# Attention: in even steps, half a projection directly behind the burst of value matmuls, not at the end of the step

## The chip, the cores and the metric

The kernel runs on one core of a Trainium2 chip. The metric is the device time of one execution in microseconds (us), from the start to the end of the program on that core; the median of several runs is compared.

## What is computed

One decoder layer in float32. Self-attention over `x` (2 x 2048 x 512, 16 heads of 32), then cross-attention to a short context, then a feed-forward network with 8 experts, each followed by a residual sum and a layer norm. Only the first of the three matters here:

```python
qkv = x @ qkv_w + qkv_b
q, k, v = ...                                   # 16 heads of 32
attn = softmax(einsum('bnhd,bmhd->bhnm', q, k) * scale)
out = einsum('bhnm,bmhd->bnhd', attn, v)
```

The output projection, the cross-attention and the experts come later in the same program and are the same before and after.

## The kernel before

The program is one long sequence for each engine, written out in Python loops, with semaphores between them. Self-attention takes the first 2,000 us or so, the rest the experts for the most part.

**Units, chunks, steps.** Four heads make a group of 128 rows, and a batch and a group make a unit: `UNITS` = 8. A unit has `NQ` = 4 chunks of 512 queries, so there are `CHUNKS` = 32 chunks. A chunk is walked in `T` = 16 steps `kt`, one for each 128 keys, and a step in `HG` = 4 turns `i`, one for each head.

**What TensorE does in a turn** (`chunk`, L781 to L804). It issues one matmul of the maxima for a chunk further on (`max_pass`, L675, tile `sa_mx`) and one matmul of scores for this chunk (`score`, L745, tile `sa_sc`). Both write 512 columns and read fp32r operands. The pass of maxima computes query by key and VectorE reduces its bank with `reduce_max` (L556), from three banks in turn. From the maxima come the shifts of the softmax: once a chunk VectorE makes them (`make_shift`, L564), TensorE transposes them into a bank of maxima in step 13 (`transpose_shift`, L683), VectorE copies them out (`leave_shift`, L576) and SyncE's queue moves them into `q_stack` for the next chunk.

**Scores.** A matmul of scores writes one of two banks in turn. ScalarE takes the exponential of each (L515, tile `sa_prob`), and score `n` waits until exponential `n - 2` is done (`after(pe, prob_ready, n - 1)`, L747).

**The burst** (`burst`, L729). In every even step, after the second score (turn 1), TensorE adds up the values of the two steps before: 8 matmuls of 32 output columns each, four of them side by side in the array (L696, tile `sa_pv`, 16 records in a trace). Where `kt % 4 == 2` four more such matmuls make the row sums of the softmax (`row_sums`, L700, tile `sa_den`, 8 records). These are float32 operands. GpSimd adds the probabilities of four steps up beforehand (L310), with VectorE's help (`add_pair`, L558).

**The projections.** While one unit is attended to, the queries, keys and values of the next are projected. One projection of 128 rows by 512 tokens is a job: 4 parts over the channels, each in `HALVES` = 2 halves, in float32. A half is one matmul of 256 columns for a query or key job (L670, 2 records) and two matmuls of 128 columns for a value job (L664, 4 records). All jobs use one PSUM bank, `misc`, one after another. Each of the 28 chunks of units 0 to 6 has three jobs (`OPS`, L110), chunks 28 and 29 have one, the last two none. Where the halves stand is written out by hand:

```python
MID, END, HALVES = 1, HG - 1, 2
SLOTS = [(kt, at) for kt in range(T) for at in ((MID, END) if kt % 2 else (END,))]
PLACES = [SLOTS[:2] + SLOTS[:6], SLOTS[7:15], SLOTS[16:24]]
```

A slot is a step and a turn; the halves of the slot are issued at the end of that turn, in an even step at `MID` behind the burst (L803 comes after L798). The three entries of `PLACES` are the places of the first, second and third job of a chunk. A finished job is read out of its bank by ScalarE (`leave_high`, L459) and VectorE (`leave_psum`, L536) at the turn in `LEFT_AT`: for the first job in step 4, for the second in step 10, for the third in step 0 of the next chunk, all in turn 1. A query or key is then moved into its stack by 12 DMAs of SyncE's queue (`move_stack`, L270). In step 13 TensorE waits before turn 0 for the stacks that chunk `g + 2` needs (L784 to L789).

**Order of the other engines.** ScalarE, VectorE and GpSimd each walk the same steps and turns in their own list; ScalarE reads the bank of values out in turn 2 of step 0 (`leave_pv`) and the bank of row sums in turn 2 of step 2 (`leave_den`). VectorE inverts the row sums in steps 8 and 12 (`invert`, L582).

Of the kernel before, what the change touches and what calls it, by code (L numbers as in the profile page):

```python
# [75 lines left out]
def self_attention(nc, z, keep, block, x, xT_dram, qkv_w, qkv_b, attnT_dram, rows_dram):  # L76


    B, N, C, KC, G, HG, D, T, NQ = z.B, z.N, z.C, z.KC, z.G, z.HG, z.D, z.T, z.NQ
# [32 lines left out]
           Op("k", 3, 1, 2, 5), Op("q", 0, 1, 2, 6), Op("v", 3, 1, 2, 5),  # L112
           Op("v", 0, 1, 3, 6), Op("q", 1, 1, 3, 7), Op("v", 1, 1, 3, 7)]
    MID, END, HALVES = 1, HG - 1, 2
    SLOTS = [(kt, at) for kt in range(T) for at in ((MID, END) if kt % 2 else (END,))]
    PLACES = [SLOTS[:2] + SLOTS[:6], SLOTS[7:15], SLOTS[16:24]]
    PLACES[0].sort()
    LEFT_AT = ((0, 4, MID), (0, 10, MID), (1, 0, MID))

# [12 lines left out]
    JOBS = [Job(0, what, n, None, None, None, None) for what, n in FIRST_OPS]  # L132
    JOBS += [Job(u + o.ahead, o.what, o.n, u * NQ + o.c, u * len(LOADS) + o.load, PLACES[i % 3], LEFT_AT[i % 3])
             for u in range(UNITS) for i, o in enumerate(OPS) if u + o.ahead < UNITS]
# [686 lines left out]
def cross_attention(nc, z, keep, block, tail, a):  # L821


    B, N, C, KC, M, E, CAP = z.B, z.N, z.C, z.KC, z.M, z.E, z.CAP
    SLOTS, NT, SKIP = z.E * z.CAP, z.TOK // P, 2 ** 20
    W = C + 2
# [18 lines left out]
    with ExitStack() as ctx:  # L845
# [272 lines left out]
        def _(pool):  # L1118
# [24 lines left out]
            def send_rows(n):  # L1143
# [8 lines left out]
                for t in range(TQ):  # L1152
                    pool.indirect_dma_start(a.rows, bass.IndirectOffsetOnAxis(ap=skip_i[:, par, t:t + 1], axis=0),
                                            x2[par][:, t, :], None, bounds_check=SLOTS - 1, oob_is_err=False).then_inc(scattered, 16)

# [1095 lines left out]
def decoder_layer(nc, x, ctx_rows, qkv_w, qkv_b, proj_w, proj_b, Wq, Wk, Wv, Wo, bo, gx, bx, gl, bl,  # L2251
                  router_w, w1, b1, w2, b2, out):
    z = Shapes(x, ctx_rows, w1)
    slots = z.E * z.CAP

    def scratch(name, shape, dt=F32):
        return nc.dram_tensor(name, shape, dt, kind="Internal").ap()

    xT = scratch("xT", (z.B, z.C, z.N))
    attnT = scratch("attnT", (z.B, z.C, z.N))  # L2260

    rows = scratch("rows", (slots, z.C + 2))
    a = Tensors()
    a.x, a.ctx, a.attnT, a.out = x, ctx_rows, attnT, out
    a.proj_w, a.proj_b, a.Wq, a.Wk, a.Wv, a.Wo, a.bo = proj_w, proj_b, Wq, Wk, Wv, Wo, bo
    a.gx, a.bx, a.gl, a.bl, a.rw = gx, bx, gl, bl, router_w
    a.w1, a.b1, a.w2, a.b2 = w1, b1, w2, b2
    a.rows = rows

    a.wqk = scratch("wqk", (z.C, z.XH * z.M))  # L2270
    a.vw = scratch("vw", (z.XH * z.M, z.C))
    with ExitStack() as ctx:
        a.counts = Stage(nc, ctx, "keep").sb("counts", [P, z.E], I32)
        with ExitStack() as keep:

            block = keep.enter_context(nc.Block())
            tail = self_attention(nc, z, keep, block, x, xT, qkv_w, qkv_b, attnT, rows)
            cross_attention(nc, z, keep, block, tail, a)
        experts(nc, z, a)
# [29 lines left out]
```

## Time and profile before

| | us |
|---|---|
| median of 3 runs (3521.16 to 3531.86) | 3529.65 |
| the profiled execution | 3527.62 |
| its span, first to last instruction | 3525.9 |
| TensorE (PE) busy, whole span | 3342.4 (95%) |
| VectorE (DVE) busy | 2646.1 (75%) |
| GpSimd (POOL) busy | 1809.5 (51%) |
| ScalarE (ACT) busy | 1703.4 (48%) |

The span and the profiled execution's own time differ by 1.7 us, which lie around the first and last instruction. PE is the stream of matmuls; their ends are modelled, so a busy PE may hold short waits, and the distance from the start of one matmul to the start of the next is the better measure. PEld are the loads of weights, which run beside matmuls. The mean granted TensorE clock is 0.976 of full speed.

### The profile page before, as it was taken

The page shows a single profiled execution, that of the slowest core. Times are in us where ns is not written, and L with a number is a line of the kernel's source. Part 1 is how long each engine was busy: PE and PEld are TensorE (multiplying, and loading weights), DVE is VectorE, ACT ScalarE, POOL GpSimd, SP SyncE. Part 2 cuts the span into 40 slices and gives each one's busy share as a digit, 9 for nine tenths or more (in the row PEclk, how much of TensorE's full clock was granted, in tenths as well). Part 3 has the DMA queues.
Part 4 walks back from the last instruction along what each step waited for, and adds up shares of the span by engine and source line. Part 5 has one row for each costly group of instructions (what it writes and reads, how often), then busy time and mean ns, then how long its engine had stood idle before and what let it go on. Part 6 is the DMA issues. An engine that isn't in the chain of part 4 may idle for free. (4 is left out here: it accounts for less than half of the span.)

```text
span 3525.9 us, 51323 instructions
## 1 busy us (share of the span) xinstructions
PE 3342.4 (95%) x18533; PEld 2356.0 (67%) x18533; DVE 2646.1 (75%) x4578; ACT 1703.4 (48%) x3101; POOL 1809.5 (51%) x884
## 2 busy tenths in 40 slices
PE   7999999999999999999999987999949999999996
PEld 6655566566666556656655445887739888988886
DVE  5888888888888888888888835888734765566667
ACT  2565665656655655656656653444312332233333
POOL 2587888888888888888888930011110101100111
PEclk9999999999999999999999998999969999999998
DMA  6321322322322322213211032132132333323332
GB/s 219 113 63 46 102 60 76 96 58 80 87 61 70 94 63 79 85 52 102 71 52 39 8 112 67 57 116 96 49 117 92 126 125 100 121 84 126 121 116 100
DMA packets 190280, 308.52 MB, mean 88 GB/s; under 512 B 25513, under 2 KB 72233, under 8 KB 190010
## 3 DMA queue, kind: packets, MB, share of 16 engines
q1 hardware_dynamic: 166970, 243.82, 22.4%
q0 software_dynamic: 14592, 44.32, 3.6%
q10 hardware_dynamic: 8448, 16.78, 1.4%
q8 instruction: 169, 2.77, 0.3%
q14 instruction: 101, 0.83, 0.1%
HBM read 195.66 MB, written 61.33 MB: 73 GB/s over the span
## 5 line engine op out<-in xcount | busy, mean ns | idle before, releaser
L556 DVE TENSOR_REDUCE sa_part_max<-sa_mx 128x1 f32<-128x512 f32 x2048 | 1311.3, 685 | 316.9 <-PE sa_mx L680 272.2
L515 ACT ACTIVATE sa_prob<-sa_sc 128x512 f32<-128x512 f32 x2010 | 1105.2, 595 | 684.9 <-PE sa_sc L748 671.0
L310 POOL TENSOR_TENSOR sa_quad_sum<-sa_quad_sum,sa_prob 128x1024 f32<-128x1024 f32 x500 | 1270.6, 2563 | 133.7 <-ACT sa_prob L515 131.8
L680 PE MATMUL sa_mx<-sa_k_even,sa_q_stack 96*128 96x512 f32 x1024 | 480.9, 473 | 15.0 <-DMA sa_q_stack<-sa_hilo 5.9
L2126 PE MATMUL ex_h<-ex_xT,ex_w 128*128 128x384 f32 (+2 forms) x2688 | 457.2, 325 | 29.6 <-issue 23.1
L680 PE MATMUL sa_mx<-sa_k_odd,sa_q_stack 96*128 96x512 f32 x1024 | 468.6, 458 | 9.8 <-DMA sa_q_stack<-sa_hilo 5.8
L2126 PEld LDWEIGHTS ex_h<-ex_xT,ex_w 128*128 128x128 f32 x2688 | 437.7, 191 | 43.6 <-issue 34.0
L310 POOL TENSOR_TENSOR sa_quad_sum<-sa_prob 128x1024 f32<-128x1024 f32 x126 | 300.2, 2383 | 234.7 <-ACT sa_prob L515 234.7
L2148 PE MATMUL ex_acc<-ex_w,ex_hT 128*128 128x512 f32 x1719 | 418.1, 394 | 0.0
L748 PE MATMUL sa_sc<-sa_q_stack,sa_k_even 98*128 98x512 f32 x1024 | 410.7, 401 | 0.0
L748 PE MATMUL sa_sc<-sa_q_stack,sa_k_odd 98*128 98x512 f32 x986 | 401.1, 409 | 1.4 <-ACT sa_prob L515 1.2
L2148 PEld LDWEIGHTS ex_acc<-ex_w,ex_hT 128*128 128x128 f32 x1719 | 319.2, 189 | 61.4
L1963 ACT ACTIVATE ex_h<-ex_h,ex_b 128x384 f32<-128x384 f32 x256 | 145.5, 580 | 345.9 <-PE ex_h L2126 345.8
L680 PEld LDWEIGHTS sa_mx<-sa_k_even,sa_q_stack 96*128 96x128 f32 x1024 | 195.5, 192 | 155.3 <-issue 101.6
L680 PEld LDWEIGHTS sa_mx<-sa_k_odd,sa_q_stack 96*128 96x128 f32 x1024 | 193.9, 189 | 152.9 <-issue 107.3
L1889 POOL DMA_DIRECT2D ex_xg<-rows x48 | 26.5, 556 | 509.0 <-PE ex_h L2111 506.9
L696 PE MATMUL sa_pv<-sa_prob,sa_v_odd 128*32 128x512 f32 x2048 | 249.1, 602 | 1.0 <-ACT sa_prob L515 1.0
L696 PE MATMUL sa_pv<-sa_prob,sa_v_even 128*32 128x512 f32 x2048 | 246.2, 598 | 0.0
L748 PEld LDWEIGHTS sa_sc<-sa_q_stack,sa_k_odd 98*128 98x128 f32 x986 | 187.0, 190 | 79.2 <-ACT sa_prob L515 55.3
L748 PEld LDWEIGHTS sa_sc<-sa_q_stack,sa_k_even 98*128 98x128 f32 x1024 | 195.1, 191 | 46.0 <-ACT sa_prob L515 19.7
L2075 DVE CAST ex_hT<-ex_h 128x384 fp32r<-128x384 f32 x256 | 94.5, 369 | 133.6 <-ACT ex_h L1963 132.9
L1141 POOL TENSOR_TENSOR ca_rstd<-ca_var_eps,ca_minus_half 128x8 f32<-128x8 f32 x16 | 26.5, 1654 | 324.4 <-DVE ca_var_eps L1209 324.4
(229 smaller groups left out, 4078.2 us busy)
## 6 DMA issues: line engine op xcount, KB each, us to landing
ex_w_in<-in_L_ffn_w_dram SPq DMA_DIRECT2D x130, 512.0 KB, 4.5
sa_xT<-xT SPq DMA_DIRECT2D x57, 1024.0 KB, 5.2
sa_q_stack<-sa_hilo SPq DMA_DIRECT2D x372, 64.0 KB, 2.0
rows<-sa_empty SPq DMA_DIRECT2D x48, 257.0 KB, 3.9
ex_rows<-rows POOLq DMA_DIRECT2D x8, 1542.0 KB, 7.7
sa_k_odd<-sa_hilo SPq DMA_DIRECT2D x192, 64.0 KB, 2.0
ex_xg<-rows POOLq DMA_DIRECT2D x48, 256.0 KB, 3.0
sa_k_even<-sa_hilo SPq DMA_DIRECT2D x168, 64.0 KB, 2.0
```

Of the source, the lines that this page charges most:

```text
L310: pool.tensor_tensor(quad_sum[:, i % 2, heads, :], so_far, prob[:, k, heads, :], ALU.add).then_inc(quad_ready, 1)
L515: act.activation(prob[:, kt % 4, j, :], score_bank(n)[:, :], ACT.Exp, scale=SCALE).then_inc(prob_ready, 1)
L556: dve.reduce_max(part_max[:, q, j, k:k + 1], max_bank(max_turn(n))[:, :], AX_X).then_inc(max_read, 1)
L680: pe.matmul(max_bank(max_turn(n))[:, :], q_stack[0:QK, j, at:at + P], k_stack[g // NQ % 2][0:QK, j, k * BANK:(k + 1) * BANK], start=True, ...
L696: last = pe.matmul(pv[D * j:D * (j + 1), :], v[buf][:, kt, D * j:D * (j + 1)], prob[:, kt % 4, j, :], start=(kt == 0), stop=(kt == T - 1))
L748: pe.matmul(score_bank(n)[:, :], k_stack[g // NQ % 2][0:AUG, j, kt * P:(kt + 1) * P], q_stack[0:AUG, j, g % NQ * BANK:(g % NQ + 1) * BANK] ...
L1141: pool.tensor_tensor(rstd[:, which, :, :], var_eps[:, which, :, :], minus_half[:, :, :], ALU.pow).then_inc(rstd_ready, 1)
L1889: pool.dma_start(xg[:, t, :], a.rows[row:row + P, 0:C]).then_inc(gathered, 16)
L1963: act.activation(h[:, j % 2, half * HALF:(half + 1) * HALF], h_bank[half][:, 0:HALF], ACT.Gelu, bias=b1[:, step:step + 1]).then_inc(h_read ...
L2075: dve.tensor_copy(hT[:, j % 2, 0, cols], h[:, j % 2, cols]).then_inc(hT_hi, 1)
L2126: last = pe.matmul(h_bank[half][:, 0:slots], w1[:, i % 2, pw, k, :], xT[:, e % 2, px, k, half * HALF:half * HALF + slots], start=(part == ...
L2148: last = pe.matmul(acc[t][:, :], hT[:, i % 2, ph, t * P:(t + 1) * P], w2[:, i % 2, pw, :], start=(i == 0 and part == 0), stop=(i == STEPS ...
```

## The change

```diff
-    SLOTS = [(kt, at) for kt in range(T) for at in ((MID, END) if kt % 2 else (END,))]
-    PLACES = [SLOTS[:2] + SLOTS[:6], SLOTS[7:15], SLOTS[16:24]]
+    SLOTS = [(kt, at) for kt in range(T) for at in ((MID, END) if kt % 2 else (MID,))]
+    PLACES = [SLOTS[1:4] + SLOTS[1:6], SLOTS[7:15], SLOTS[16:24]]
     PLACES[0].sort()
```

The slots of even steps go from turn 3 to turn 1, where they stand behind the burst. Written out, with (step, turn):

| job | places before | places after |
|---|---|---|
| first | (0,3) (0,3) (1,1) (1,1) (1,3) (2,3) (3,1) (3,3) | (1,1) (1,1) (1,3) (1,3) (2,1) (2,1) (3,1) (3,3) |
| second | (5,1) (5,3) (6,3) (7,1) (7,3) (8,3) (9,1) (9,3) | (5,1) (5,3) (6,1) (7,1) (7,3) (8,1) (9,1) (9,3) |
| third | (11,1) (11,3) (12,3) (13,1) (13,3) (14,3) (15,1) (15,3) | (11,1) (11,3) (12,1) (13,1) (13,3) (14,1) (15,1) (15,3) |

No instruction, wait or DMA is added or removed. The last half of every job stays where it was, and so do the turns at which the jobs are read out.

## Rows read from the trace of the kernel before

**Rows 1.** The page: TensorE's busy tenths in 40 slices of 88 us.
```profile
PE   7999999999999999999999987999949999999996
```

**Rows 2.** Timeline of TensorE, the bursts of chunk 9: start us, us, engine, line, operation.
```profile
670.60 1.92 PE L696 MATMUL sa_pv<-sa_prob,sa_v_even 128*32 128x512 f32 x16
...
678.56 1.92 PE L696 MATMUL sa_pv<-sa_prob,sa_v_even 128*32 128x512 f32 x16
...
686.53 1.92 PE L696 MATMUL sa_pv<-sa_prob,sa_v_even 128*32 128x512 f32 x16
...
693.46 1.92 PE L696 MATMUL sa_pv<-sa_prob,sa_v_even 128*32 128x512 f32 x16
...
701.42 1.93 PE L696 MATMUL sa_pv<-sa_prob,sa_v_even 128*32 128x512 f32 x16
...
708.52 1.92 PE L696 MATMUL sa_pv<-sa_prob,sa_v_even 128*32 128x512 f32 x16
...
716.34 1.93 PE L696 MATMUL sa_pv<-sa_prob,sa_v_even 128*32 128x512 f32 x16
...
724.56 1.92 PE L696 MATMUL sa_pv<-sa_prob,sa_v_even 128*32 128x512 f32 x16
...
732.54 1.92 PE L696 MATMUL sa_pv<-sa_prob,sa_v_even 128*32 128x512 f32 x16
```

**Rows 3.** Timeline behind the burst of step 6 of chunk 9: a half at (6,3).
```profile
695.20 1.04 PE L704 MATMUL sa_den<-sa_quad_sum,sa_ones 128*32 128x512 f32 x8
...
696.17 0.19 PEld L680 LDWEIGHTS sa_mx<-sa_k_even,sa_q_stack 96*128 96x128 f32 x1 [0.84 <-issue]
696.17 0.50 PE L680 MATMUL sa_mx<-sa_k_even,sa_q_stack 96*128 96x512 f32 x1
...
696.51 0.39 PE L748 MATMUL sa_sc<-sa_q_stack,sa_k_even 98*128 98x512 f32 x1
...
696.98 0.40 PE L748 MATMUL sa_sc<-sa_q_stack,sa_k_even 98*128 98x512 f32 x1
...
697.21 0.59 PE L670 MATMUL sa_misc<-sa_xT,sa_wkv 128*128 128x256 f32 x2
...
697.88 0.40 PE L748 MATMUL sa_sc<-sa_q_stack,sa_k_even 98*128 98x512 f32 x1
```

**Rows 4.** Timeline behind the burst of step 10 of chunk 9: no half at (10,3).
```profile
712.01 2.28 ACT L515 ACTIVATE sa_prob<-sa_sc 128x512 f32<-128x512 f32 x4 [2.19 <-PE sa_sc L748]
712.05 0.40 PE L748 MATMUL sa_sc<-sa_q_stack,sa_k_even 98*128 98x512 f32 x1
...
712.66 0.19 PEld L748 LDWEIGHTS sa_sc<-sa_q_stack,sa_k_even 98*128 98x128 f32 x1 [0.42 <-ACT sa_prob L515]
712.67 0.51 PE L748 MATMUL sa_sc<-sa_q_stack,sa_k_even 98*128 98x512 f32 x1
...
713.25 0.40 PE L748 MATMUL sa_sc<-sa_q_stack,sa_k_even 98*128 98x512 f32 x1
```

**Rows 5.** Waits between 184 and 1948 us: waiter, releaser, us in total, times, longest.
```profile
PEld sa_sc L748 <- ACT sa_prob L515: 46.5, 153, 0.4
...
PE sa_mx L680 <- DMA sa_q_stack<-sa_hilo: 9.6, 14, 1.6
```

**Rows 6.** Timeline of VectorE and TensorE in steps 12 to 14 of chunk 9.
```profile
716.01 0.39 PE L748 MATMUL sa_sc<-sa_q_stack,sa_k_even 98*128 98x512 f32 x1
...
720.68 2.57 DVE L556 TENSOR_REDUCE sa_part_max<-sa_mx 128x1 f32<-128x512 f32 x4
...
723.16 0.67 DVE L580 CAST sa_shiftT<-sa_mx 8x512 fp32r<-8x512 f32 x1
...
723.89 0.50 PE L680 MATMUL sa_mx<-sa_k_even,sa_q_stack 96*128 96x512 f32 x1 [0.22 <-DVE sa_shiftT L580]
```

**Rows 7.** Timeline at step 13, turn 0 of chunk 11.
```profile
843.61 0.61 PE L664 MATMUL sa_misc<-sa_wkv,sa_xT 128*128 128x128 f32 x4
...
844.45 0.50 PE L680 MATMUL sa_mx<-sa_k_odd,sa_q_stack 96*128 96x512 f32 x1 [0.23 <-DMA sa_q_stack<-sa_hilo]
```

## The prediction

> **What bounds the kernel now.** First the page: TensorE is busy nine tenths or more in nearly every slice of self-attention [rows 1], so the length of this stage is what TensorE issues, plus the short waits between its matmuls that this digit can't show. So the next view is the timeline of TensorE, and in it the distance from burst to burst, since a half moves within such a period of two steps. Chunk 9 has bursts at 670.60, 678.56, 686.53, 693.46, 701.42, 708.52, 716.34, 724.56 and 732.54 us [rows 2], so the periods that begin with steps 0, 2, 4, ... 14 take 7.96, 7.97, 6.93, 7.96, 7.10, 7.82, 8.22 and 7.98 us. Each has the same 16 matmuls of maxima and scores and the same 8 of values; steps 2, 6, 10 and 14 have row sums besides, and the halves number 5, 3, 2, 3, 3, 2, 3, 3.
>
> The third view is what a half costs where it stands. Two scores without a half between them are 0.47 us apart (696.51, 696.98), with a half 0.90 (697.88) [rows 3], so a half takes **0.43** of TensorE's stream. Yet the period of step 8 (three halves) is only 0.17 longer than that of step 4 (two, none in turn 3 of the even step), and step 6 only 0.14 longer than step 10, the same pair with row sums [rows 2]. So a half at the end of an even step costs 0.14 to 0.17 net, and **0.26 to 0.29 us of it is cover for something else**. The timeline behind burst 10 shows what: the scores run 712.05, 712.67, 713.25, so 1.20 us for two distances where 0.94 would be TensorE's own pace, and the load of the first waits for an exponential [rows 4]. ScalarE needs 0.57 for one (2.28 for 4) against TensorE's 0.47 for a score and a maximum, and there are two banks; behind a burst the first two scores go out freely and the next two wait. A half in turn 3 of the even step stands exactly there and gives ScalarE the time. The list of waits has this one 153 times [rows 5]; it is small now because only steps 4 and 10 lack the half, and where no half comes at all.
>
> **The change, part by part.** Nothing is added or removed. The sum is over a chunk of 28 with three jobs.
>
> *The moved half itself.* Behind the burst it costs x, which no row shows. A burst ends with a hole: the row sums start at 695.20, 8 records of which four run together, and the next matmul at 696.17, 0.97 later, where two groups at the 0.43 of those in the burst would be 0.86; the score after it comes 0.34 later instead of 0.23 [rows 3]. I take it that the half meets the hole as the maximum does: its first record waits the 0.11, its second comes 0.34 later instead of 0.22, and the maximum behind it then follows at the normal pace. The hole is paid once, as before, and x = 0.43 + 0.01 to 0.02 = **0.45**. Bounds: if the hole's two parts (0.11 and 0.10) took the half in, x = 0.22; if a value job's four small records each met a late load once more, the 0.11 again, x = 0.56. I take 0.45, which is nearest the row of the maximum behind a burst.
>
> The row of the load is to be weighed against a rule. The load for the maximum behind the burst starts at 696.17 with its matmul, after 0.84 idle [rows 3]: it wasn't pulled ahead. The Trainium skill ("TensorE: Matmul & The Clock Gate", Part 2, what happens when you issue a matmul) says that the engine pulls weight loads ahead of running matmuls when they go to the background buffer. By that the half's load would be done by the end of the burst, and the total near the second rival's below; the trace does not agree for a load behind this burst.
>
> *Steps 6, 8, 14: one half each from turn 3 to behind the burst.* What is left between bursts is the period with two halves: 6.93 without row sums (step 4), 7.80 with (step 10, 7.82, or 6.93 + 0.86 = 7.79). Plus x: step 6 becomes 8.25 against 7.96, **+0.29**; step 8 7.38 against 7.10, **+0.28**; step 14 8.26 against 7.98, **+0.28**. What covered the moved half's time was ScalarE's lag, and that cover stays behind as a wait. Behind the burst ScalarE has long run dry (2.19 idle, [rows 4]), and so has VectorE, so the half covers nothing there.
>
> *Steps 0 and 2, the first job.* Two halves leave (0,3), one goes to (1,3), one to (2,1), and (2,3) goes to (2,1). Step 0 then holds four halves, all in step 1: 6.93 + 2 x 0.43 = 7.79 against 7.96, **-0.17**: a half less, and the wait is back. Step 2 holds two in the stretch and two behind the burst: 7.80 + 0.45 + 0.43 = 8.68 against 7.97, **+0.71**. ScalarE's reading of the row sums in that step ends no later than now.
>
> *Step 12.* Here VectorE leads in half of the chunks: its reductions run without a break, four in 2.57 us, then the copy of the shifts at 723.16, and TensorE's maximum at 723.89 waits for it [rows 6]. That chain starts with the first maximum behind the burst, as VectorE has run dry by then, so it moves by the whole of x: **+0.45**. In the other half TensorE waits before (13,0) for a stack's DMAs, 14 times in 28 chunks [rows 5]; in chunk 11 it could go on at 843.61 + 0.36 and goes on at 844.45, 0.48 later [rows 7]. The half at (12,3) and the half at (12,1) both lie ahead of this point, the DMAs start from step 10, which is unchanged, so the arrival moves by x - 0.43 only: **0**. Mean +0.22.
>
> *Queues and other waits.* The DMAs of the stacks, loads and shifts hang on the last halves and on the shifts. The former don't move; the shifts come up to 0.45 later in step 13 and are wanted two steps on, some 8 us. GpSimd's additions get more time, not less. Cost nothing. The first half of a first job waits for the bank at (1,1) instead of (0,3), later, so no new wait.
>
> *Sum:* 0.29 + 0.28 + 0.28 - 0.17 + 0.71 + 0.22 = 1.61 us a chunk, 28 times 45.1, and 2 x 0.54 for chunks 28 and 29, together **46 us**. On the profiled execution's 3527.62 that is 3574; this execution lies 2 us under the median of 3529.65, so 3574 to 3576. I say 3575.
>
> As a function of x a chunk changes by 4.5 x - 0.42: steps 2, 6, 8 and 14 hold one x each, step 12 half of one, and the second half of the pair in step 2 costs 0.43 whatever the hole. It breaks even at x = 0.09.
>
> **Rivals.**
> *The half fills the hole.* The weight load of a full-width float32 half is ready when the burst ends, and the two delays of 0.11 and 0.10 vanish in it: x = 0.22 to 0.24. Then 28 x (4.5 x 0.23 - 0.42) = 17 us, plus 1: about **3546**. For it: burst and half are both float32, the maxima are not. Against it: a half between two fp32r matmuls shows no delay at either change (0.90 - 0.47 is 0.43, two records at some 0.22 each), so it isn't the type that makes the hole but the change of width, which stays. Even if the 0.33 from the last score to the burst (716.01 [rows 6] to 716.34 [rows 2]) shrank to the usual 0.23 as well, x would be 0.13 and the end 3533. 10%.
> *The other side: no loss, or a gain.* The two periods in which I read the lag, those of steps 4 and 10, are also the ones in whose first turns ScalarE reads out a finished job besides its exponentials. If the late scores come of that and not of the missing half, the other steps have no lag to give back: steps 6, 8 and 14 change by x - 0.43 = +0.02 each, steps 0 and 2 together by as much, step 12 by up to half of 0.02. That is 28 x 0.1 = 3 us, **3531**, no change; with the hole filled too, 28 x 4.5 x 0.20 = 25 us less, 3503. It decides where ScalarE is still busy with the job when the first score behind the burst lands. Against it: it sat idle for 2.19 us before its first exponential behind burst 10 [rows 4], so the read was long over. 4%.
> *Dearer than forecast.* Each half behind a burst meets a second late load, above all the value jobs (three of four third jobs, steps 12 and 14), x = 0.56: 28 x 4.5 x 0.11 = 14; and the waits for stacks do not absorb step 12, 14 x 0.45 = 6 more: up to **3595**. 13%.
> That the change doesn't do what it says is excluded by the table of places; but note that the first job's two halves from step 0 don't all go behind a burst, and half of them go to step 1.
>
> **How the numbers follow.** My case 73%: x from 0.43 to 0.48, and the lag from 0.24 to 0.30, give 3568 to 3583. The range takes in part of the other cases: up to 3596, and down to 3553, since x may lie between hole and no hole in only some of the steps. A measurement of this kernel can tell about 0.3%, 10.6 us, from no change. Faster by over that needs both the hole and no lag, 2%; within it, the opposite rival by itself and the lower edge of the first, 5%; slower 93%.
>
> **What would show it.** In the timeline of the changed kernel: (1) step 8's period about 7.38 and step 6's 8.25; (2) behind each even burst the half's first record about 0.54 after the last group of values starts, its second 0.34 after that; (3) the third and fourth score behind every burst late, and the wait of score loads for exponentials about 300 to 400 times instead of 153; (4) step 0 shorter by 0.17, step 2 longer by 0.7; (5) the waits for stacks at (13,0) as now, 14 times. I am wrong if the period with a half behind the burst is within 0.05 of the present one: then either x is near 0.2 or ScalarE's lag was not the cover.

## The result, and the profile after

The changed kernel takes 3572.86 us (median of 4 runs, 3572.76 to 3576.62), the kernel before in the same session 3526.28 us (4 runs): ratio **1.013**, 95% interval 1.0117 to 1.0143, 46.6 us slower. The forecast was 3575 us, 3553 to 3596, slower. TensorE's granted clock was 1.00 in chunks 1 to 27 in both traces, so the clock has no part in the difference.

The page shows as little of it as before. Its line of TensorE's busy time, and the line of slices:

```profile
span 3571.1 us, 51323 instructions
...
PE 3387.2 (95%) x18533; PEld 2327.2 (65%) x18533; DVE 2624.6 (73%) x4578; ACT 1703.6 (48%) x3101; POOL 1807.3 (51%) x884
...
PE   7999999999999999999999987999949999999997
```

The same 18533 matmuls are "busy" 45 us longer. The record of a matmul of scores or maxima lasts some 0.40 us, and the next one is due 0.23 after its start, so a score that starts 0.14 late (0.61 after the last one instead of 0.47, as below) leaves no gap in the busy time. The starts of the bursts say more. TensorE's timeline of chunk 9, the counterpart of [rows 2]:

```profile
687.75 1.92 PE L696 MATMUL sa_pv<-sa_prob,sa_v_even 128*32 128x512 f32 x16
...
695.54 1.92 PE L696 MATMUL sa_pv<-sa_prob,sa_v_even 128*32 128x512 f32 x16
...
704.19 1.92 PE L696 MATMUL sa_pv<-sa_prob,sa_v_even 128*32 128x512 f32 x16
...
711.12 1.92 PE L696 MATMUL sa_pv<-sa_prob,sa_v_even 128*32 128x512 f32 x16
...
719.36 1.92 PE L696 MATMUL sa_pv<-sa_prob,sa_v_even 128*32 128x512 f32 x16
...
726.73 1.92 PE L696 MATMUL sa_pv<-sa_prob,sa_v_even 128*32 128x512 f32 x16
...
734.55 1.92 PE L696 MATMUL sa_pv<-sa_prob,sa_v_even 128*32 128x512 f32 x16
...
743.23 1.92 PE L696 MATMUL sa_pv<-sa_prob,sa_v_even 128*32 128x512 f32 x16
...
751.49 1.92 PE L696 MATMUL sa_pv<-sa_prob,sa_v_even 128*32 128x512 f32 x16
```

The periods are 7.79, 8.65, 6.93, 8.24, 7.37, 7.82, 8.68 and 8.26 us, against 7.96, 7.97, 6.93, 7.96, 7.10, 7.82, 8.22 and 7.98. Steps 4 and 10 stand still, every other one has moved. What happens inside is in the timeline behind the burst of step 8, which now has its half in front:

```profile
721.21 0.30 PEld L670 LDWEIGHTS sa_misc<-sa_xT,sa_wkv 128*128 128x128 f32 x2 [0.84 <-issue]
721.21 0.70 PE L670 MATMUL sa_misc<-sa_xT,sa_wkv 128*128 128x256 f32 x2
721.53 0.19 PEld L680 LDWEIGHTS sa_mx<-sa_k_even,sa_q_stack 96*128 96x128 f32 x1
721.56 0.59 PE L680 MATMUL sa_mx<-sa_k_even,sa_q_stack 96*128 96x512 f32 x1
...
721.99 0.39 PE L748 MATMUL sa_sc<-sa_q_stack,sa_k_even 98*128 98x512 f32 x1
...
722.42 1.78 ACT L515 ACTIVATE sa_prob<-sa_sc 128x512 f32<-128x512 f32 x3 [2.33 <-PE sa_sc L748]
722.46 0.39 PE L748 MATMUL sa_sc<-sa_q_stack,sa_k_even 98*128 98x512 f32 x1
...
723.07 0.19 PEld L748 LDWEIGHTS sa_sc<-sa_q_stack,sa_k_even 98*128 98x128 f32 x1 [0.42 <-ACT sa_prob L515]
723.07 0.50 PE L748 MATMUL sa_sc<-sa_q_stack,sa_k_even 98*128 98x512 f32 x1
...
723.64 0.42 PE L748 MATMUL sa_sc<-sa_q_stack,sa_k_even 98*128 98x512 f32 x1
```

Three things are to be seen. The load of the half starts with its first record, after the same 0.84 idle that the maximum's load had [rows 3]: nothing is pulled into the burst. The first score comes 2.63 after the burst's start (721.99 - 719.36), where in the kernel before it came 2.19 (718.53 against 716.34 in step 12 of chunk 9), so the half costs 0.44 in this place. In step 8 itself the kernel before has the same 2.19 (703.61 against the burst's 701.42 in [rows 2]):

```profile
703.61 0.39 PE L748 MATMUL sa_sc<-sa_q_stack,sa_k_even 98*128 98x512 f32 x1
```

And the third score is 0.61 behind the second and the fourth 0.57 behind the third, as in [rows 4]: the lag is back. In the list of waits, 184 to 1948 us as in [rows 5]:

```profile
PEld sa_sc L748 <- ACT sa_prob L515: 130.8, 430, 0.4
...
PE sa_mx L680 <- DMA sa_q_stack<-sa_hilo: 9.0, 14, 1.5
```

The wait for exponentials is there 430 times instead of 153, 277 more, although this stretch of time holds less than before of chunks 28 and 29, where the wait is frequent in both kernels. Over chunks 1 to 27 alone the traces have it 404 times against 108: two more in each of five periods of every chunk (0, 2, 6, 8 and 14), and 26 in all in step 12. The wait for DMAs is as it was, 14 times.

### The profile page after: what moved, and what is told of

Read it like the earlier page. It is cut to its first block and busy times, and to the rows that moved or that the text cites. A ratio compares the mean times of both kernels' runs of the same rounds, so it can differ in the third digit from the quotient of the medians.

```text
span 3571.1 us, 51323 instructions
## 1 busy us (share of the span) xinstructions
PE 3387.2 (95%) x18533; PEld 2327.2 (65%) x18533; DVE 2624.6 (73%) x4578; ACT 1703.6 (48%) x3101; POOL 1807.3 (51%) x884
## 5 line engine op out<-in xcount | busy, mean ns | idle before, releaser
L556 DVE TENSOR_REDUCE sa_part_max<-sa_mx 128x1 f32<-128x512 f32 x2048 | 1297.5, 684 | 379.2 <-PE sa_mx L680 347.2
L680 PE MATMUL sa_mx<-sa_k_even,sa_q_stack 96*128 96x512 f32 x1024 | 471.1, 464 | 15.3 <-DMA sa_q_stack<-sa_hilo 6.0
L680 PE MATMUL sa_mx<-sa_k_odd,sa_q_stack 96*128 96x512 f32 x1024 | 460.1, 449 | 9.7 <-DMA sa_q_stack<-sa_hilo 5.6
L748 PE MATMUL sa_sc<-sa_q_stack,sa_k_even 98*128 98x512 f32 x1024 | 422.2, 412 | 0.0
L748 PE MATMUL sa_sc<-sa_q_stack,sa_k_odd 98*128 98x512 f32 x986 | 409.3, 417 | 1.5 <-ACT sa_prob L515 1.5
```

The lines of the kernel that those rows point to most:

```text
L556: dve.reduce_max(part_max[:, q, j, k:k + 1], max_bank(max_turn(n))[:, :], AX_X).then_inc(max_read, 1)
L680: pe.matmul(max_bank(max_turn(n))[:, :], q_stack[0:QK, j, at:at + P], k_stack[g // NQ % 2][0:QK, j, k * BANK:(k + 1) * BANK], start=True, ...
L748: pe.matmul(score_bank(n)[:, :], k_stack[g // NQ % 2][0:AUG, j, kt * P:(kt + 1) * P], q_stack[0:AUG, j, g % NQ * BANK:(g % NQ + 1) * BANK] ...
```

## The experiments

The kernels are compared with the kernel before as it ran beside them: 3525.77 us for the two parts, the half ahead of the burst and the half left out; 3524.96 for the short exponentials and the quarters first; 3524.32 for the half in turn 2 and the half first. All are read by the same measure, the mean length of each period over chunks 1 to 27, worked out from the starts of the bursts in each trace (in us; the last column is the start of chunk 28 less that of chunk 1):

| kernel | 0 | 2 | 4 | 6 | 8 | 10 | 12 | 14 | chunks 1-27 |
|---|---|---|---|---|---|---|---|---|---|
| before | 7.98 | 7.97 | 6.93 | 7.95 | 7.10 | 7.82 | 8.73 | 7.99 | 1686.4 |
| after | 7.81 | 8.67 | 6.93 | 8.22 | 7.37 | 7.81 | 8.97 | 8.26 | 1729.1 |
| second and third jobs only | 7.98 | 7.97 | 6.93 | 8.22 | 7.37 | 7.81 | 8.81 | 8.26 | 1710.2 |
| first job only | 7.80 | 8.67 | 6.93 | 7.95 | 7.10 | 7.81 | 8.57 | 7.99 | 1696.1 |
| half ahead of the burst | 8.68 | 7.79 | 7.37 | 8.23 | 6.93 | 8.26 | 8.93 | 7.81 | 1727.8 |
| half at (8,3) left out | 7.98 | 7.97 | 6.93 | 7.95 | 6.93 | 7.82 | 8.70 | 7.99 | 1681.2 |
| short exponentials, old places | 7.98 | 8.08 | 6.70 | 8.08 | 7.10 | 7.59 | 8.83 | 7.99 | 1683.4 |
| short exponentials, new places | 7.59 | 8.44 | 6.70 | 8.08 | 7.14 | 7.58 | 8.90 | 8.03 | 1686.3 |
| half in turn 2 | 8.23 | 8.21 | 6.93 | 8.20 | 7.34 | 7.81 | 8.80 | 8.24 | 1721.3 |
| nine places, quarters first | 7.97 | 7.97 | 6.75 | 7.95 | 7.10 | 7.62 | 8.74 | 7.99 | 1676.1 |
| nine places, half first | 7.97 | 7.97 | 6.75 | 7.95 | 7.10 | 7.62 | 8.74 | 7.99 | 1676.2 |

Each row is one trace. The column of step 12 has a scatter of its own: in the half of the chunks that wait for DMAs it is 8.9 to 9.4 on average, from trace to trace, which alone moves the last column by up to 7 us. The start of chunk 1 lies between 170.3 and 175.2 us, in kernels whose programs differ little up to there.

### The change in two parts

```diff
+    BEHIND = [(kt, at) for kt in range(T) for at in ((MID, END) if kt % 2 else (MID,))]
-    PLACES = [SLOTS[:2] + SLOTS[:6], SLOTS[7:15], SLOTS[16:24]]
+    PLACES = [SLOTS[:2] + SLOTS[:6], BEHIND[7:15], BEHIND[16:24]]
```

> Only the second and third job of each chunk take the places behind the bursts; the first job keeps its old ones. Theory A (ScalarE's lag: a half in turn 3 of an even step covers 0.27 us of the wait for exponentials, and the same half behind the burst costs 0.44): steps 6, 8 and 14 longer by 0.26 to 0.28 each, step 12 by 0.43 in half of the chunks and 0 in the other half, so 1.0 us a chunk, 28 us, ratio to the kernel before 1.008. Theory B (the loss is of the first job, whose halves crowd in steps 1 and 2): no difference here, ratio 1.000 to 1.002.

3550.74 us, ratio 1.007 (1.0053 to 1.0087), 25 us. The other part, with `BEHIND` as above:

```diff
+    PLACES = [BEHIND[1:4] + BEHIND[1:6], SLOTS[7:15], SLOTS[16:24]]
```

> Only the first job takes its new places. Theory A: step 0 shorter by 0.17, step 2 longer by 0.70, so 0.53 a chunk, 16 us over 30 chunks, ratio 1.0045, and with the run of the other two jobs alone it adds up to the whole change. Theory B: nearly the whole loss is here, 40 us or more, ratio 1.011 to 1.013.

3540.28 us, ratio 1.0045 (1.0031 to 1.0059), 14.5 us. Each part moves its own periods, by as much as in the whole change, and no other; 25 and 14.5 make 39.5 of the 46.6; each part's interval reaches some 5 us to either side, so the 7 us between are not shown to be an effect. By period the parts add up for all but step 12, whose DMA waits differ between the traces. The loss is not one of the crowded first job alone: of the 39.5 us, five eighths come from the second and third job, which move single halves.

### The half ahead of the burst

```diff
                     score(g, kt, i)
+                    if kt % 2 == 0:
+                        for job, part in PARTS_AT.get((g, kt, i), ()):
+                            project_part(job, part)
                     if g < LAST or kt <= 2:
...
-                    for job, part in PARTS_AT.get((g, kt, i), ()):
-                        project_part(job, part)
+                    if kt % 2:
+                        for job, part in PARTS_AT.get((g, kt, i), ()):
+                            project_part(job, part)
```

> The changed kernel, but in even steps the half is issued ahead of the burst (behind the score of turn 1) instead of behind it. Theory A: neither place is where the scores lag, so the time is that of the changed kernel within 3 us, 3570 to 3576, with step 8 at 7.35 to 7.40 us. Theory C (what costs is that every engine that has run dry in the burst starts later by the half): ScalarE and VectorE work on during a half ahead of the burst, they start at once behind it, and most of the 46 us is gone: 3530 to 3540, step 8 near 7.1.

3571.6 us, ratio 1.0124 (1.0107 to 1.0141), the time of the changed kernel. My number for step 8 missed by bad bookkeeping: a half ahead of burst 8 counts in the period that begins with burst 6. So step 6 (with (8,1)) is 8.23, step 4 (with (6,1)) is 6.93 + 0.44 = 7.37, and step 8 is 6.93 without any. What the other engines do while TensorE is at the half makes no difference; that it isn't in turn 3 does.

### A half left out

```diff
         for part, at in enumerate(job.place or ()):
+            if at == (8, END):
+                continue
```

> The kernel before, with the half at (8,3) of each second job left out of the projection (its 256 columns lack one of four channel parts). Theory A: step 8 falls from 7.10 only to 6.93, by 0.17, although a half is 0.43 of the stream; the wait of score loads for exponentials rises by about 56 times; 28 chunks give 4 to 5 us less. Theory D (the lag in steps 4 and 10 comes of ScalarE reading out a job there, so other steps have none): step 8 falls by the whole 0.43 to 6.67, 12 us less.

Step 8 falls to 6.93, and the waits rise by 58, from 153 to 211. So work of 0.43 us, taken from an engine that in the kernel before is busy for 1671.01 of the 1686.40 us of chunks 1 to 27, was worth 0.17. Those chunks get 5.2 us shorter, where 27 x 0.17 is 4.6; the whole program ran once, in 3524.19 us, too near 3525.77 to tell. No job is read out in step 8, so the lag isn't a matter of steps 4 and 10: that is the rival of the other side gone. TensorE's timeline of chunk 9, bursts 8 and 10:

```profile
702.11 1.92 PE L698 MATMUL sa_pv<-sa_prob,sa_v_even 128*32 128x512 f32 x16
...
709.04 1.92 PE L698 MATMUL sa_pv<-sa_prob,sa_v_even 128*32 128x512 f32 x16
```

### Short exponentials, at the old and at the new places

```diff
-   act.activation(prob[:, kt % 4, j, :], score_bank(n)[:, :], ACT.Exp, scale=SCALE).then_inc(prob_ready, 1)
+   act.activation(prob[:, kt % 4, j, 0:BANK // 2], score_bank(n)[:, 0:BANK // 2], ACT.Exp, scale=SCALE).then_inc(prob_ready, 1)
```

The same edit is made to the kernel before and to the changed one. Both leave out half of every exponential, so they serve for the timing only.

> The kernel before with each exponential cut to 256 of its 512 columns (the other 256 keep old contents, so the attention is wrong); the places are the old ones. It takes the lag away by making ScalarE fast, some 0.35 us for one. Theory A: periods with a half at turn 3 stay (step 8 7.10, step 6 7.96), those without fall by 0.26 (step 4 to 6.67, step 10 to 7.54). Rival (the late scores come of VectorE's maxima or of the weight loads): step 4 stays at 6.93.

> The changed kernel with the same short exponentials. Theory A: without the lag a half costs its 0.43 to 0.44 in either place, so step 8 comes to 7.10 to 7.12 instead of 7.37, and chunks 1 to 27 take the same time as with short exponentials and the old places within 3 us. Rival (the place behind the burst is dear in itself): the difference of 1.6 us a chunk, 43 us over chunks 1 to 27, stays, step 8 at 7.37.

An exponential now takes 0.385 us instead of 0.595. One run each, 3496.70 us and 3500.15. At the old places the two periods without a half in turn 3 fall by 0.23, the others with the lag covered don't gain. At the new places the six moved periods come down, step 8 to 7.14, and chunks 1 to 27 take 1686.3 us against 1683.4: of the **42.7 us that the change costs, 2.9 are left**. This is the run that decides: the same places, the same holes behind the bursts, and only the exponential shorter. The 2.9 flatter the case somewhat. Steps 2 and 6 were to stay at 7.97 and 7.96 at the old places and both went to 8.08, by another effect (last section), which lengthens the old-places kernel by 27 x (0.11 + 0.13) = 6.5 us. The periods that this effect leaves alone are the better witness: steps 8 and 14 lost 0.27 each by the change with full exponentials, and 0.04 each with short ones. A half costs about what it takes in either place, and nearly all of the loss was the lag. A little lag stays, too: step 4, which has one half less than step 8, takes 6.70 instead of 7.10 - 0.43 = 6.67. The timeline behind burst 8 of chunk 9 with short exponentials and the new places:

```profile
705.95 0.39 PE L748 MATMUL sa_sc<-sa_q_stack,sa_k_even 98*128 98x512 f32 x1
...
706.38 1.82 ACT L515 ACTIVATE sa_prob<-sa_sc 128x256 f32<-128x256 f32 x4 [2.56 <-PE sa_sc L748]
706.41 0.39 PE L748 MATMUL sa_sc<-sa_q_stack,sa_k_even 98*128 98x512 f32 x1
...
706.81 0.19 PEld L748 LDWEIGHTS sa_sc<-sa_q_stack,sa_k_even 98*128 98x128 f32 x1 [0.20 <-ACT sa_prob L515]
706.89 0.42 PE L748 MATMUL sa_sc<-sa_q_stack,sa_k_even 98*128 98x512 f32 x1
```

The third score is 0.48 behind the second instead of 0.61, nearly TensorE's own pace, but its load still waits for the first exponential. An exponential of 0.385 can't be too slow for a score every 0.47. Nor does ScalarE work without a break in the changed kernel when the full exponentials make TensorE wait. Three narrow windows of its timeline behind burst 8 of chunk 9 show the first three starts:

```profile
722.42 0.60 ACT L515 ACTIVATE sa_prob<-sa_sc 128x512 f32<-128x512 f32 x1 [2.33 <-PE sa_sc L748]
...
722.91 0.59 ACT L515 ACTIVATE sa_prob<-sa_sc 128x512 f32<-128x512 f32 x1
...
723.61 0.60 ACT L515 ACTIVATE sa_prob<-sa_sc 128x512 f32<-128x512 f32 x1
```

The second starts 0.49 after the first, before that one has ended; then ScalarE sits idle from 723.50 to 723.61, because the third score itself came late (723.07). So ScalarE can take an exponential every 0.49, close to TensorE's 0.47, and has time to spare while TensorE waits for a bank. What is waited for is the **round trip of a bank**: from the start of a score to the start of its exponential 0.43 (705.95, 706.38), then the exponential. With 0.60 that is 1.03, and the load of the score two on starts some 0.05 later, at 1.08, and its matmul with it; it would be wanted at 0.94. With 0.385 it is 0.82, and the load is at 0.86, in time for a matmul at 0.94. So the rows put the lag down to the round trip over two banks, and not to ScalarE's pace.

### The half in turn 2

```diff
-    SLOTS = [(kt, at) for kt in range(T) for at in ((MID, END) if kt % 2 else (END,))]
+    SLOTS = [(kt, at) for kt in range(T) for at in ((MID, END) if kt % 2 else (END - 1,))]
```

> The kernel before with the halves of even steps in turn 2 instead of turn 3, between the first and the second score behind the burst. Theory A (two banks; the third score waits for the first exponential, the fourth for the second): a half there leaves the third score free, but the fourth still comes one bank too early, so the wait of 0.14 us and the late weight load of 0.10 behind it return at the fourth: step 8 at 7.33 to 7.38, ratio 1.008 to 1.012. Rival (any place in the stretch gives ScalarE the time): step 8 at 7.10 to 7.15, ratio under 1.002.

3565.17 us, ratio 1.0115 (1.0099 to 1.013), step 8 at 7.34. One turn too early costs 41 us, nearly as much as the change's 46.6. The timeline behind burst 8 of chunk 9 shows the wait one score later, at the fourth:

```profile
714.28 0.40 PE L748 MATMUL sa_sc<-sa_q_stack,sa_k_even 98*128 98x512 f32 x1
714.51 0.59 PE L670 MATMUL sa_misc<-sa_xT,sa_wkv 128*128 128x256 f32 x2
...
715.18 0.39 PE L748 MATMUL sa_sc<-sa_q_stack,sa_k_even 98*128 98x512 f32 x1
...
715.65 0.40 PE L748 MATMUL sa_sc<-sa_q_stack,sa_k_even 98*128 98x512 f32 x1
...
716.26 0.19 PEld L748 LDWEIGHTS sa_sc<-sa_q_stack,sa_k_even 98*128 98x128 f32 x1 [0.41 <-ACT sa_prob L515]
716.26 0.50 PE L748 MATMUL sa_sc<-sa_q_stack,sa_k_even 98*128 98x512 f32 x1
```

The half covers only what is wanted right after it.

### Nine places for a job

Steps 4 and 10 lack the half in turn 3 because a job has eight halves and nine places. Here two places get a quarter each:

```diff
-    PLACES = [SLOTS[:2] + SLOTS[:6], SLOTS[7:15], SLOTS[16:24]]
+    PLACES = [SLOTS[:2] + SLOTS[:6], SLOTS[6:15], SLOTS[15:24]]
+    QUARTERS = 2 * HALVES
+    PLACES[0] = [at for at in PLACES[0] for _ in range(2)]
+    PLACES[1:] = [[at for n, at in enumerate(places) for _ in range(2 if n > 1 else 1)] for places in PLACES[1:]]
...
```

The rest of the edit makes `project_part` take any run of quarters. Quarters of one job that stand in the same turn go out as one piece, so the two halves at (0,3) of a query or key job, for one, are now one matmul.

> The kernel before, but the second and third job use nine places instead of eight, (4,3) and (10,3) too: the first two places get a quarter each (128 columns, or one of the two matmuls of a value), the other seven a half. The same work. Theory A: a quarter of 0.22 us in turn 3 covers most of the lag of 0.26, so step 4 goes from 6.93 to 6.70 to 6.75 and step 10 from 7.80 to 7.57 to 7.62; what step 10 gains is eaten by the wait for DMAs in step 13 in half of the chunks; 8 to 10 us less in all, ratio 0.9975. Rival (the lag is spread along the stretch, or small pieces cost more than they cover): ratio 1.000 or over.

3519.79 us against 3524.96, ratio **0.9982** (0.9973 to 0.9991). Step 4 is 6.75 and step 10 7.62, as forecast. Chunks 1 to 27 are 10.3 us shorter in the trace, the whole program 5.2 in the medians (interval 3.2 to 9.5). Where the other 5 us go is not shown; outside chunks 1 to 27 the traces with full exponentials differ by up to 5.7 us (1839.4 to 1845.1). It is a small gain, but it beats both kernels.

> As the run with quarters, but of the nine places the first, (4,3) and (10,3), gets a whole half and the two after it a quarter each. Theory A: the whole half covers the whole lag at the third score, a quarter of 0.22 suffices between the later pairs (ScalarE needs 1.14 for a pair, TensorE 0.94 + 0.22), so step 4 at 6.67 to 6.70 against 6.75 with the quarter first, step 10 at 7.54 to 7.58; 10 us less than the kernel before, ratio 0.997. Rival: the quarters leave a lag at their own places, step 4 at 6.75 or over.

The variant puts the whole half first and the quarters behind it (`1 if n in (1, 2) else 2`): 3519.79 us against 3524.32, again 0.9982, and step 4 again 6.75, not 6.67 to 6.70. Theory A missed here, and the rival's number holds. The timeline of this variant in steps 4 and 5 of chunk 9, with a quarter ahead of 691.42 and another ahead of 692.62:

```profile
691.42 0.42 PE L755 MATMUL sa_sc<-sa_q_stack,sa_k_even 98*128 98x512 f32 x1
...
691.83 0.19 PEld L755 LDWEIGHTS sa_sc<-sa_q_stack,sa_k_even 98*128 98x128 f32 x1 [0.19 <-ACT sa_prob L523]
691.91 0.41 PE L755 MATMUL sa_sc<-sa_q_stack,sa_k_even 98*128 98x512 f32 x1
...
692.62 0.40 PE L755 MATMUL sa_sc<-sa_q_stack,sa_k_even 98*128 98x512 f32 x1
...
693.01 0.19 PEld L755 LDWEIGHTS sa_sc<-sa_q_stack,sa_k_even 98*128 98x128 f32 x1 [0.19 <-ACT sa_prob L523]
693.10 0.41 PE L755 MATMUL sa_sc<-sa_q_stack,sa_k_even 98*128 98x512 f32 x1
```

A pair of scores takes 1.19 us (691.91 to 693.10). I had set 1.14 for a pair, half of four exponentials in 2.28, which has ScalarE's idle time between two pairs only once. TensorE's own 0.94 + 0.22 = 1.16 falls short of 1.19, so about 0.03 is lost at each of the two pairs with a quarter. That is most of the 0.08 by which 6.75 lies over 6.67.

## Why the prediction was right

The total (3575 against 3572.86) is right by its own steps, not by luck. Per period, forecast and measured mean of chunks 1 to 27: step 0 -0.17 and -0.17; step 2 +0.71 and +0.70; step 6 +0.29 and +0.28; step 8 +0.28 and +0.27; step 12 +0.22 and +0.24; step 14 +0.28 and +0.27. That is 1.61 and 1.58 a chunk; chunks 28 and 29 grew by 0.58 and 0.56, where 0.54 was forecast.

- *x.* Taken as 0.45 between 0.22 and 0.56; it is 0.44, and the value jobs cost no more: burst to first score 2.64 against 2.19 in step 12 of chunk 9. The first rival, which wanted it at 0.23, falls by that, and by the row of the half's load: it starts after 0.84 idle, with its own matmul. So the rule that the prediction takes from the Trainium skill ("TensorE: Matmul & The Clock Gate", Part 2), weight loads pulled ahead of running matmuls, does not show for a load behind this kind of burst.
- *The lag.* Read off as the difference between periods with and without the half in turn 3. Shown three ways: left out, the half gives back only 0.17; with short exponentials the loss falls from 42.7 to 2.9 us, and in steps 8 and 14 from 0.27 to 0.04; and in any other place, behind the burst, ahead of it or one turn early, it returns.
- *Step 12.* In the chunks where VectorE leads, 8.21 became 8.65, against +0.45 forecast. In the 14 others the mean went from 9.21 to 9.26, against 0. That is not quite one case: in the six with long waits the mean stood still (10.10 and 10.07), but in the eight with short ones, chunk 11 of [rows 7] among them, 8.54 became 8.65, the length of the chunks where VectorE leads, so VectorE's chain most likely ends last there now. The forecast left out this crossing; it is worth 0.03 a chunk.
- *Right in size, wrong in its reason.* The cause of the lag was put as ScalarE's 0.57 for an exponential against 0.47. The 0.57 is a misreading of [rows 4]: 2.28 for four is one row of the timeline, which swallows the short idle time between two pairs. With a bank ready, the exponentials start 0.49 apart. The size was right, as it came from the periods, but the term behind it was not: it is the round trip of one of two banks, 1.19 for a pair against 0.94. The number of waits, 430, lies above my 300 to 400: two more in each of five periods, over 27 chunks, are 270, and with the 153 that already makes 423. And a cover "for something else" was reckoned as if all or nothing; the quarters show that it is taken in parts.
- *Not tried.* A third bank for the scores, which by this account should remove the lag in all places at once: the kernel's eight banks (two for scores, three for maxima, one each for values, row sums and projections) are all in use, and one taken from the maxima would change VectorE's round trip as well. That the round trip and not ScalarE is the limit rests on the two runs with short exponentials and on the rows, not on such a run.

## What to carry to other kernels

An engine that the profile shows busy 99% of the time can still have stalls that a piece of its own work hides: before moving that piece, compare periods that have it with periods that don't, and take the difference, not the piece's length, as what it costs where it stands. The right place for such filler is just ahead of the instruction that would wait, and here it was sharp: one turn early cost 41 us where the far place cost 46.6. Where two buffers go round, add up the whole round trip (start of the producer to start of the consumer, the consumer, the release) and set it against the producer's time for two.

## What the runs showed of the hardware

Going from full-width matmuls to a burst and back had a price that didn't depend on what came next. Behind a burst of 32-column matmuls, four side by side, the first full-width one came 0.11 us later than the pace, and the second 0.10 later. The first load started only with its matmul, and the second load behind it. Ahead of a burst it is about 0.10 more (716.01 to 716.34, [rows 6] and [rows 2], against 0.23). A float32 half and an fp32r maximum met the same, so the type of what follows doesn't matter; whether it is the width or the four side by side, no run separates.

VectorE and GpSimd got in each other's way in an addition from SBUF. With short exponentials and the old places, GpSimd's came first in step 6 of chunk 9 and VectorE's took 3.41 us; in the kernel before, VectorE's came first and took 1.22, and GpSimd's was stretched instead. The timeline with short exponentials, then that of the kernel before:

```profile
695.36 2.37 POOL L310 TENSOR_TENSOR sa_quad_sum<-sa_quad_sum,sa_prob 128x1024 f32<-128x1024 f32 x1 [0.30 <-ACT sa_prob L515]
695.40 3.41 DVE L562 TENSOR_TENSOR sa_quad_sum<-sa_prob 128x1024 f32<-128x1024 f32 x1
```

```profile
694.07 1.22 DVE L562 TENSOR_TENSOR sa_quad_sum<-sa_prob 128x1024 f32<-128x1024 f32 x1
694.27 3.26 POOL L310 TENSOR_TENSOR sa_quad_sum<-sa_quad_sum,sa_prob 128x1024 f32<-128x1024 f32 x1 [0.30 <-ACT sa_prob L515]
```

In both orders the one that began second ended about its own length after the first one's end: VectorE's 1.08 us after (1.22 alone), GpSimd's 2.24 after (2.37 alone). So the second one waits out the first. The Trainium skill ("SBUF — State Buffer", Terms) says that the two engines share a port pair which one instruction holds to its end; the rows agree. With short exponentials VectorE's addition took 3.4 us in steps 2 and 6 of every chunk from 1 to 27. At the old places TensorE's loads then waited for VectorE's reductions far more often (184 to 1948 us; first with short exponentials, then the kernel before):

```profile
PEld sa_mx L680 <- DVE sa_part_max L556: 30.6, 100, 0.9
```

```profile
PEld sa_mx L680 <- DVE sa_part_max L556: 2.9, 15, 0.3
```

So this is the likely reason why a faster ScalarE made steps 2 and 6 longer, 8.08 instead of 7.97 and 7.95: it let GpSimd start first, VectorE's reductions began late, and TensorE waited for a bank of maxima. It is read from the traces; no run tests it alone.
